# A retention layer with an FP4 feed-forward on one core: state in halves of 64 tokens, one-instruction rotation, first layernorm's sum on TensorE, and every engine's program written out call by call

## The reference

```python
q = rope((x @ Wq).reshape(b, l, NH, DQK)); k = rope(...)          # rotation of feature pairs
decay = jnp.where(diff >= 0, jnp.exp2(diff[None] * s[:, None, None]), 0.0)
scores = jnp.einsum('bhqd,bhkd,hqk->bhqk', q * DQK ** (-0.5), k, decay)
o = jnp.einsum('bhqk,bhkd->bhqd', scores, v)
o = o * jax.lax.rsqrt(jnp.mean(o * o, axis=-1, keepdims=True) + EPS) * g_norm_w
o = o.reshape(b, l, VDIM) * (g * jax.nn.sigmoid(g))
x = _layernorm(x + o @ Wo)
def fp4_linear(x, w): return einsum('bsk,nk->bsn', fp4_quant_dequant(x), fp4_quant_dequant(w))
h = jax.nn.silu(fp4_linear(x, w_gate)) * fp4_linear(x, w_up)      # 352 wide
x = _layernorm(x + fp4_linear(h, w_down))
```

## Time and profile before

| | |
|---|---|
| median of 3 runs | 137.76 us |
| profiled execution: span from first to last instruction | 135.8 us |
| profiled execution: own time, as span and 2.0 us around it | 137.8 us |
| PE busy | 121.6 us (90%) |
| DVE busy | 112.9 us (83%) |
| ACT busy | 98.0 us (72%) |
| POOL busy | 96.6 us (71%) |
| granted TensorE clock, mean | 0.999 |
| read from and written to memory | 5.26 MB, 1.05 MB |

### The profile page before, as it was taken

The page is one execution under the profiler, slowest core; times in us unless marked ns, Lnnn a source line. Parts: engine busy times, 40 slices in busy tenths (PEclk is TensorE's granted clock), DMA queues, the critical chain, the costliest instruction groups (busy, mean ns, idle before and its releaser), DMA issues.

```text
span 135.8 us, 3550 instructions
## 1 busy us (share of the span) xinstructions
PE 121.6 (90%) x1248; PEld 79.6 (59%) x1248; DVE 112.9 (83%) x391; ACT 98.0 (72%) x311; POOL 96.6 (71%) x139
## 2 busy tenths in 40 slices
PE   4997998999999999999999999999999958888660
PEld 4755574755656566575758584848484745445450
DVE  1269889876879899999999999999999899999710
ACT  3055665778858787787888888888888978876753
POOL 4212856878677778878787979797979697656561
PEclk9999999999999999999999999999999999999999
DMA  3899980000000000000000000000000000000011
GB/s 105 262 250 237 409 288 5 7 2 0 5 0 0 5 0 2 0 7 0 0 5 0 0 7 19 0 19 7 19 0 24 0 19 19 22 19 19 27 54 59
DMA packets 6897, 6.53 MB, mean 48 GB/s; under 512 B 864, under 2 KB 6112, under 8 KB 6752
## 3 DMA queue, kind: packets, MB, share of 16 engines
q1 hardware_dynamic: 5856, 5.56, 13.6%
q10 hardware_dynamic: 1024, 0.76, 1.7%
HBM read 5.26 MB, written 1.05 MB: 46 GB/s over the span
## 4 chain that ended last, share of the span: by engine, by line
PE 75%; DVE 11%; ACT 8%; issue 3%; POOL 2%; POOLq 1%; DVEq 0%; ACTq 0%
PE ps L338 12%; PE ps L357 7%; PE ps L485 6%; PE ps L469 6%; PE ps L462 5%; PE ps L397 5%; PE ps L329 4%; PE ps L387 4%; PE ps L476 3%; PE ps L370 3%; PE ps L405 3%; PE ps L422 2%; PE ps L421 2%; PE ps L413 2%; PE ps L323 2%
## 5 line engine op out<-in xcount | busy, mean ns | idle before, releaser
L902 POOL TENSOR_TENSOR rstd_h<-ms,minus_half 128x8 f32<-128x8 f32 x16 | 26.4, 1647 | 7.7 <-DVE ms L767 7.0
L893 POOL TENSOR_TENSOR qk<-rope_c,rope_s 128x256 f32<-128x256 f32 x16 | 11.6, 726 | 13.0 <-DVE rope_s L744 12.9
L338 PE MATMUL ps<-w_vg,xT_sb 128*128 128x512 f32 x32 | 18.0, 645 | 0.0
L485 PE MATMUL ps<-wd_T,hT 128*128 128x128 f32 x96 | 13.6, 278 | 2.7 <-ACT hT L515 2.7
L927 POOL TENSOR_TENSOR hq<-h_grid,hs 128x352 f32<-128x352 f32 x16 | 13.0, 812 | 3.0 <-DVE h_grid L680 3.0
L516 ACT ACTIVATE q_eo<-ps,consts 128x128 f32<-128x128 f32 x32 | 11.8, 369 | 3.4 <-PE ps L347 3.4
L485 PEld LDWEIGHTS ps<-wd_T,hT 128*128 128x128 f32 x96 | 12.1, 193 | 3.5 <-DVE r L794 2.6
L740 DVE TENSOR_TENSOR rope_c<-ps,tabs_sb 128x256 f32<-128x256 f32 x16 | 6.8, 425 | 8.8 <-PE ps L329 8.8
L515 ACT ACTIVATE raw<-ps 128x512 f32<-128x512 f32 x16 | 9.6, 599 | 5.9 <-PE ps L357 5.9
L897 POOL TENSOR_SCALAR_AFFINE_SELECT probs<-raw 128x512 f32<-128x512 f32 x16 | 10.3, 642 | 4.7 <-ACT raw L515 4.6
L469 PE MATMUL ps<-wgu_T,xqT 128*128 128x352 f32 x32 | 12.4, 469 | 0.2
(11 more groups left out here) (112 smaller groups left out, 363.1 us busy)
## 6 DMA issues: line engine op xcount, KB each, us to landing
tabs_sb<-rope_tables SPq DMA_DIRECT2D x1, 1024.0 KB, 10.8
out<-x SPq DMA_DIRECT2D x16, 64.0 KB, 1.5
tabs_sb<-rope_tables SPq DMA_DIRECT2D x1, 640.0 KB, 7.3
xT_sb<-x_transposed SPq DMA_DIRECT2D x1, 512.0 KB, 8.7
...
```

Source lines behind the costliest of these rows:

```text
L338: mm(vg_ps, xT(c), w_vg[:], start=True, stop=True).then_inc(vg_pe, 1)
L485: last = mm(down_ps, hT[:, c % 2, t, :], wd_T[:, t, :], start=t == 0, stop=t == 2)
L893: gp.tensor_tensor(qk[:, c % D, :], rope_c[:, c % D, :], rope_s[:, c % D, :], ALU.add).then_inc(qk_p, 1)
L902: gp.tensor_tensor(rstd_h[:, c, :], ms[:, c, :], minus_half[:], ALU.pow).then_inc(rms_p, 1)
```

## The change

What it does, part by part:

- **Halves.** `C` stays 128 for all projections and for the feed-forward, but the recurrence runs on halves of `CH = 64` tokens. `scores` becomes eight products (pair of heads by half) on tiles of 32 rows by 64 columns, 128 columns moving; keys and queries of different halves are never multiplied. `state_product` becomes eight products (pair by half, 64 rows deep), `from_state` sixteen with 64 columns moving, and `values` sixteen, 64 rows deep with 64 columns moving. `next_state` runs twice a chunk. The masked scores are 128 by 512 values in all, so VectorE masks all of them in one instruction, and `copy_scores` (ScalarE) and `mask_scores` on GpSimd go.
- **Rotation.** The tables hold cosines and signed sines for all 256 columns (4H columns a chunk in place of 2H). VectorE multiplies `qk` by both in one instruction with 128 by 512 results, and GpSimd adds the two with the halves of each pair swapped in its read.
- **First layernorm.** `Wo` is centred over its columns once (`centre_wo`), and `out_projection` gets a third product, x transposed times the centring matrix, so that PSUM holds the centred sum of residual and attention. `ln1_sum`, `ln1_stats`, `ln1_aggr`, `ln1_centre` and the load of `x_res` go; ScalarE's `ln1_squares` (with its accumulator read) and `ln1_norm` read PSUM.
- **Buffers and banks.** Most buffers have `D = 4` copies, the ratio buffers six; `plus` and `grid` write in place. The PSUM banks are dealt anew (`BANKS`).
- **Order.** The stage loops go; each engine's list of calls is written out.

```diff
-        FIRST, LAST = -2, 28
-        def stage_runner(s): ...
+        BANKS = {"sc": (0, 1, 2, 3), "oT": (0, 1, 2, 3), "o": (3,), "yT": (2,), "qk": (4,), "qkT": (6,),
+                 "vg": (5,), "att": (5,), "xqT": (6,), "gate": (1,), "hT": (4,), "up": (7,),
+                 "down": (0,), "U": (6, 7)}
 def scores(c):
-    for j in range(NP):
-        last = mm(sc_ps(j), kT[rows, c % D, :], q_eo[rows, c % D, :, :]..., start=True, stop=True)
+    for a in range(2):
+        for j in range(NP):
+            last = mm(sc_ps(j)[CH * a:CH * a + CH, :], kT[rows, c % D, CH * a:CH * a + CH],
+                      q_eo[rows, c % D, a, :, :]..., start=True, stop=True)
 def state_product(c):
     for j in range(NP):
+        for a in range(2):
+            keys = slice(CH * a, CH * a + CH)
+            last = mm(U_ps(a)[32 * j:32 * j + 32, :], qk[keys, ...], v_sb[keys, ...], start=True, stop=True)
 def from_state(c):
+    for a in range(2):
         for n in range(NH):
-            mm(oT_ps[...], S[rows, c % 2, ...], q_eo[rows, c % D, e, :], start=True, stop=False)
+            mm(oT_bank(n // 4, a)[...], S[rows, (2 * c + a) % 8, ...], q_eo[rows, c % D, a, e, :], ...)
 def values(c):
     for n in range(NH):
+        for a in range(2):
+            keys = slice(CH * a, CH * a + CH)
+            last = mm(oT_bank(n // 4, a)[...], v_sb[keys, ...], probs[keys, c % D, n, :], start=False, stop=True)
 def out_projection(c):
+    mm(att_ps, xT(c), centring[:], start=True, stop=False)
-    mm(att_ps, yT[:, c % 2, 0, :], wo_s[:, 0, :], start=True, stop=False)
+    mm(att_ps, yT[:, c % D, 0, :], wo_c[:, 0, :], start=False, stop=False)
...
 def rotate(c):
-    vec.tensor_tensor(g16(rope_c[...]), g16(qk_ps), t, ALU.mult)
-    vec.scalar_tensor_tensor(g16(rope_s[...])[:, :, 0, :], g16(qk_ps)[:, :, 1, :], -1.0, sin, ...)
-    vec.tensor_tensor(g16(rope_s[...])[:, :, 1, :], g16(qk_ps)[:, :, 0, :], sin, ALU.mult)
+    vec.tensor_tensor(rope[:, c % D, :, :], qk_ps.unsqueeze(1).to_broadcast([128, 2, 256]),
+                      tabs(c).rearrange("p (t n) -> p t n", t=2), ALU.mult).then_inc(rope_v, 1)
+def centre_wo():
+    vec.tensor_reduce(wo_sum[:], wo_s[:], AX.X, ALU.add)
+    vec.scalar_tensor_tensor(wo_c[:], wo_sum[:]..., -1.0 / H, wo_s[:], ALU.mult, ALU.add)
+def ln1_squares(c):
+    nc.scalar.activation(r1_sq[...], att_ps, ACT.Square, scale=H ** -0.5, accum_out=var1[:, c, :])
...
+x_inv(8); h_ratio_(6); x_ratio_(8); next_state(13, 0); h_grid_(5); next_state(13, 1); h_plus_(6)   # DVE
```

More of the change, by code:

```diff
@@ L15 @@
 C = 128
+CH = C // 2
 NC = T // C
@@ L35 @@
 LEAST = 6e-12
-LN = ["sum", "stats", "aggr", "eps"]
 QUANT = ["amax", "inv", "ratio", "plus", "grid"]
@@ L318, in warm_up, with occupy @@
+            def occupy(name, banks):
+                for n in banks:
+                    free(n)
+                    tile[n] = name
+                filled[name] += 1
             def warm_up(n):
@@ L484, in down @@
                 for t in range(3):
[L485 removed]
+                    last = mm(down_ps, hT[:, c % D, t, :], wd_T[:, t, :], start=t == 0, stop=t == 2)
                 last.then_inc(down_pe, 1)
[L487 to L510 removed]
+            warm_up(4); project_qk(0); warm_up(4); project_vg(0); transpose_qk(0); warm_up(4); project_vg(1)
@@ new lines, in _ @@
+            project_qk(6); project_vg(6); scores(3); transpose_qk(4); project_qk(7); from_state(3); values(3)
+            state_product(4); out_projection(1); transpose_xq(0); project_qk(8); transpose_o(3); gate(0)
+            transpose_qk(5); transpose_y(2); project_vg(7); scores(4); project_qk(9); from_state(4); state_product(5)
+            values(4); out_projection(2); up(0); transpose_xq(1); transpose_o(4); transpose_y(3); gate(1)
+            transpose_qk(6); project_vg(8); scores(5); project_qk(10); from_state(5); state_product(6); values(5)
@@ new lines, in _ @@
+            out_projection(3); transpose_o(5); transpose_y(4); transpose_xq(2); up(1); gate(2); project_qk(11)
+            transpose_qk(7); scores(6); project_vg(9); from_state(6); state_product(7); values(6); project_qk(12)
+            transpose_o(6); transpose_qk(8); transpose_y(5); up(2); scores(7); out_projection(4); state_product(8)
+            from_state(7); values(7); project_qk(13); transpose_xq(3); transpose_o(7); transpose_y(6); gate(3)
+            transpose_qk(9); project_vg(10); scores(8); project_qk(14); state_product(9); from_state(8); values(8)
@@ new lines, in _ @@
+            out_projection(5); transpose_o(8); up(3); transpose_y(7); project_qk(15); transpose_qk(10); scores(9)
+            project_vg(11); transpose_xq(4); from_state(9); values(9); state_product(10); out_projection(6)
+            transpose_o(9); gate(4); transpose_y(8); up(4); transpose_qk(11); scores(10); project_vg(12)
+            transpose_xq(5); from_state(10); values(10); state_product(11); out_projection(7); transpose_o(10)
+            gate(5); transpose_y(9); up(5); transpose_qk(12); scores(11); project_vg(13); transpose_xq(6)
@@ new lines, in _ @@
+            from_state(11); values(11); state_product(12); out_projection(8); transpose_o(11); gate(6)
+            transpose_y(10); up(6); transpose_qk(13); scores(12); project_vg(14); transpose_xq(7); from_state(12)
+            values(12); state_product(13); out_projection(9); transpose_o(12); gate(7); transpose_y(11); up(7)
+            transpose_qk(14); scores(13); project_vg(15); transpose_xq(8); from_state(13); values(13)
+            state_product(14); out_projection(10); transpose_o(13); transpose_y(12); gate(8); up(8); transpose_qk(15)
@@ new lines, in _ @@
+            scores(14); out_projection(11); transpose_xq(9); from_state(14); values(14); state_product(15)
+            transpose_h(0); transpose_o(14); gate(9); up(9); transpose_y(13); out_projection(12); transpose_xq(10)
+            transpose_h(1); down(0); gate(10); up(10); transpose_xq(11); scores(15); transpose_h(2); up(11); down(1)
+            gate(11); transpose_h(3); transpose_y(14); out_projection(13); down(2); transpose_h(4); from_state(15)
+            values(15); transpose_h(5); transpose_xq(12); transpose_o(15); down(3); gate(12); up(12); transpose_h(6)
```

748 lines of the change are left out of this document (341 added, 407 removed).

## The result

The changed kernel takes 136.86 us (median of 7 runs, 136.03 to 137.35) where the kernel before takes 137.76 beside it. The ratio is 0.992, 95% interval 0.989 to 0.995. The forecast was 126.5, its range 120.5 to 136.5: the direction came true, the size did not; 10.4 us are missing.

The account below looks back on a forecast made before the run. PE was taken to bound the middle, with DVE next after 0.3 us. Head 27.5, middle 65 and tail 30.5 made 123; gaps of 1.5 and 2.0 us around the span gave 126.5 us, range 120.5 to 136.5.

Parts of the forecast that it names:

- DVE would be next at once: Full stages of the middle: taking work off PE or DVE alone moves the bound to the other after 0.3 us.
- PE's price: TensorE per chunk: small products fall from 1.70 to about 1.33 us, out_projection adds 0.22, stage 6.74 to about 6.6.
- Rival 1: Small MATMULs on PE cost by number, 26.6 ns each: +0.8 to +1.2 us a chunk, 139.5 to 145 us; chance 0.14.
- rival 4: PE tiles no longer run eight at once: +0.5 us a chunk, about 130 us; chance 0.18 shared with rival 2.
- the sum of 5.98 us a chunk: VectorE's work: 6.41 us less 0.14 for rotation and 0.49 for first layernorm, plus 0.20 for the second state update.
- Neither was the bound and both fall further from it, so I count nothing: POOL loses 642 ns and ACT 599 ns a chunk; no effect on the time was counted for this.
- Middle: Mask of chunk 3 to mask of chunk 15, 12 stages: 65 us plus 1.5 us for gaps, against 77.5 before.
- The two allowances above the 63: Middle, above PE's 63 us: taking the larger of PE and DVE stage by stage gives 65, gaps add 1.5.
- Head: Start to the mask of chunk 3: 27.5 us from DVE's work, a weight wait and 0.2 for tables, against 26.45 before.
- Tail: From the mask of chunk 15 to the end: 30.5 us including 1.3 for gaps, against 31.9 before.
- rival 2: The fixed list makes engines wait 0.3 to 0.5 us a stage, or tables land late: 131 to 134; chance 0.18 with rival 4.
- The signs I had named: Mask of chunk 15 near 93 us; after 98 with PE full, PE's price is wrong; gaps on PE and DVE blame the list.

Follow-up runs that it names:

- the reordered kernel: The changed kernel with only GpSimd's list of the same 112 calls in another order: 132.46 us, ratio 0.962 to the kernel before.

## Why the prediction was right in its direction and wrong in its size

- **What bounds.** Right for before: PE held the middle (the rotation alone changed nothing, 0.9989). That DVE would be next at once holds only with the contention (chain 49% DVE). Without it PE bounds again (84%), and DVE has 4.3 us to spare in the middle.
- **PE's price.** The small products were forecast at 1.33 us a chunk and took 1.45, 15 ns a MATMUL; the pace in `values` is 0.29 us for 32 MATMULs, 9 ns each. Rival 1 (26.6 ns) is refuted by these rows. So is rival 4: `values` takes 0.29 instead of 0.55, and `scores` 0.41 instead of 0.64. The Trainium skill (TensorE: Matmul & The Clock Gate, section "Wait — 56ns, not 53.3ns?") has a floor of about 25 ns from start to start; for tiles that run side by side this trace does not agree, with 9 ns over 32 MATMULs.
- **DVE's price.** The rotation was right (676 ns against 0.68 us), and GpSimd's sum takes the 0.73 us that were named where nothing holds it (mean 0.77). **The step that failed is the sum of 5.98 us a chunk**, together with the sentence on POOL and ACT, "Neither was the bound and both fall further from it, so I count nothing". It took the six quantisation steps at their lengths in a kernel where GpSimd rarely held them and where a hold cost no time. In their place the changed kernel has 540 ns a chunk of waiting inside them, 8.6 us on DVE, and 6.6 us of time. With the reads taken away DVE is busy 106.5 us, where the forecast's count had 107, so the sum was right but for this term. POOL matters although it is busy for only 68% of the span and has 5% of the chain. The forecast should have asked which instructions of the two engines exclude each other, and where the new lists put them side by side.
- **Middle.** 66.5 forecast, 67.02 with the contention gone, 71.41 with it. That the first two agree to 0.5 us is partly luck. DVE's work was right (62 counted, 62.72 measured), but PE is busy 66.39 us where 63 were counted, 1.4 of it from the price of the small products and the rest not broken down. The two allowances above the 63, 2 us for uneven stages and 1.5 us for gaps, made up for it: the gaps are 0.6 us.
- **Head.** 27.5 forecast, 30.09 measured, 29.33 without contention. It was summed from DVE's work, 20.2 us, and one wait of 2.1 us. The work was right (19.6). The waits are 5.2 us instead of 2.1: 1.26, 2.28, 0.85 and 0.39 us in the rows above and one of 0.28. The mask of chunk 3 is more than 1 us late, but its wait is for PE and not for a transfer, so the tables are not the cause; the first rotation starts at 5.31 here and at 4.98 in the reordered kernel, with the same loads, against 4.95 before. Of the 2.6 us, 0.76 is the slow start of this execution.
- **Tail.** 30.5 forecast, 33.6 measured, 31.75 without contention, which added 1.85. The 1.25 that are left go with more work than was counted: without contention PE is busy 26.67 us in the tail where 25.1 were counted, and DVE 24.02 where 22.9 were. All of PE's work was counted at 108 us, and it is busy 118.9 without contention; the same count (16 x 6.74 + 3) gives 111 for the kernel before, where PE is busy 121.6. So there was probably less room outside the middle than the forecast thought.
- **Rivals.** The measured time lies between rival 2 (131 to 134) and rival 1 (139.5 to 145), in neither. Rival 2 is half right: the list does not fit. But its mechanism was engines that wait, and in the profile both are busy. The signs I had named, "later than 98 with PE full, PE's price is wrong; if PE and DVE both have gaps, the list is", fit neither case: mask 15 at 101.5, PE busy 68.6 of 71.4 us, and PE's price off by only 0.12 us a chunk.

The ledger, from the profiled spans, for 135.1 - 124.5 = 10.6 us: contention 6.2 (4.4 in the middle, 1.85 in the tail, shown by taking it away), slow start of the profiled execution 0.8, head 1.8, tail 1.25, middle 0.5. Against the medians it is 136.86 - 126.5 = 10.4 us, with 6.6 from taking GpSimd's reads away. What else could shorten the tail of 31.75 was not tried.
